# A state-space block with a mixture of experts on one core: the tail work of a unit is reordered, sums of squares move to ScalarE, and the end of the kernel is arranged anew

## What is computed

```python
x = x + conv(ln_c(x))        # conv: layer norm, mamba block, layer norm, projection
t = x as 4096 tokens
t = t + moe(ln_t(t))

def mamba(x):                # d_inner 128, state 16, 4 taps
    xi, z = split(x @ in_proj_w.T)
    xs = silu(causal_conv(xi)); dt, B, C = split(xs @ x_proj_w.T)
    delta = softplus(dt @ dt_proj_w.T + b)
    h[n] = exp(delta * A[n]) * h[n] + delta * xs * B[n]      # along 1024 tokens
    y = sum_n h[n] * C[n] + D * xs
    return (y * silu(z)) @ out_proj_w.T

def moe(x):                  # 8 experts, 640 places each, top 1
    e = argmax(x @ gate_w + gate_b); place = running count within e
    y = relu(x @ w1[e] + b1[e]) @ w2[e] + b2[e]
    return y * prob * (place < 640)
```

## Time and profile before

| | us |
|---|---|
| median of 3 runs | 411.19 (409.86 to 411.86) |
| the profiled execution, its own time | 404.2 |
| its span, first to last instruction | 402.4 |
| VectorE busy | 316.0 (79%) |
| TensorE busy | 314.5 (78%) |
| GpSimd busy | 269.3 (67%) |
| ScalarE busy | 225.2 (56%) |

### The profile page before, as it was taken

How to read it: one execution, slowest core, us unless ns; L and a number is a source line. 1 busy time by engine, 2 the same in 40 slices (tenths; PEclk the granted TensorE clock), 3 DMA queues, 4 the chain that set the end, 5 groups by cost and what they waited for, 6 DMA issues and landing times. The chain is left out here.

```text
span 402.4 us, 4213 instructions
## 1 busy us (share of the span) xinstructions
PE 314.5 (78%) x1257; PEld 187.1 (47%) x1257; DVE 316.0 (79%) x355; ACT 225.2 (56%) x398; POOL 269.3 (67%) x196
## 2 busy tenths in 40 slices
PE   8832988647988799898888959877678759999930
PEld 3311433113634355473434426544366536989920
DVE  4799998999997968999797899999997223565650
ACT  4456688718676944857885846455533226464410
POOL 3436847988564797688659768966588500777771
PEclk9975799998899955969996896999999559999975
DMA  5186999989987866588975638999801063000000
GB/s 105 29 290 242 266 294 402 374 201 377 368 261 285 241 197 252 195 247 280 329 241 187 222 135 281 284 329 340 156 21 31 15 189 81 9 16 17 21 11 0
DMA packets 43985, 78.67 MB, mean 195 GB/s; under 512 B 16051, under 2 KB 26094, under 8 KB 43963
## 3 DMA queue, kind: packets, MB, share of 16 engines
q1 hardware_dynamic: 41066, 73.88, 57.4%
q0 software_dynamic: 2896, 4.53, 4.0%
HBM read 72.30 MB, written 7.54 MB: 198 GB/s over the span
## 5 line engine op out<-in xcount | busy, mean ns | idle before, releaser
L481 POOL TENSOR_TENSOR prod<-h,csb 128x1024 f32<-128x1024 f32 (+1 forms) x64 | 142.0, 2221 | 55.5 <-DVE h L1217 33.4
L1217 DVE TENSOR_TENSOR_SCAN h<-dA,Bp 128x1024 f32<-128x1024 f32 (+1 forms) x64 | 137.7, 2151 | 4.8 <-ACT hl L661 1.4
L910 PE MATMUL Yp<-prod,ident 128*128 128x512 f32 (+1 forms) x256 | 128.3, 633 | 16.1 <-POOL prod L481 16.0
L647 ACT ACTIVATE dA<-delta,aneg 128x1024 f32<-128x1024 f32 (+1 forms) x64 | 69.0, 1090 | 29.8 <-DVE h L1217 25.5
L910 PEld LDWEIGHTS Yp<-prod,ident 128*128 128x128 f32 x256 | 50.0, 209 | 73.9 <-issue 46.5
L1187 DVE TENSOR_TENSOR Bp<-Cp,bsb 128x1024 f32<-128x1024 f32 (+1 forms) x64 | 74.6, 1166 | 3.5 <-DMA bsb<-bc_rows 1.4
L562 POOL DMA_INDIRECT out_dram<-dA,csb x30 | 30.7, 1023 | 28.1 <-DVE dA L1404 20.8
L520 POOL DMA_INDIRECT slots<-rows_,slot x30 | 30.1, 1005 | 7.2 <-issue 4.5
L1390 DVE TENSOR_TENSOR dA<-Bp,b2s 128x320 f32<-128x320 f32 x8 | 3.9, 491 | 26.2 <-PE Bp L1081 26.2
L1071 PE MATMUL Cp<-prod,w1s 128*128 128x384 f32 (+1 forms) x64 | 21.5, 459 | 0.0
L1081 PEld LDWEIGHTS Bp<-w2s,prod 128*128 128x128 f32 x160 | 19.0, 192 | 1.4 <-ACT prod L814 1.0
(11 more groups left out here) (276 smaller groups left out, 552.1 us busy)
## 6 DMA issues: line engine op xcount, KB each, us to landing
bsb<-bc_rows SPq DMA_DIRECT2D x48, 512.0 KB, 5.6
csb<-bc_rows SPq DMA_DIRECT2D x48, 512.0 KB, 5.8
bsb<-bc_rows SPq DMA_DIRECT2D x16, 384.0 KB, 4.7
csb<-bc_rows SPq DMA_DIRECT2D x16, 384.0 KB, 5.7
slots<-fill POOLq DMA_DIRECT2D x1, 2600.0 KB, 21.8
csb<-slots SPq DMA_DIRECT2D x6, 325.0 KB, 5.4
bcs<-bc_rows SPq DMA_DIRECT2D x2, 512.0 KB, 12.3
xs_in<-in_x_dram SPq DMA_DIRECT2D x1, 768.0 KB, 5.5
```

Source lines behind the costliest of these rows:

```text
L481: po.tensor_tensor(prod[:, k % 4, c], h[:, k % 3, c], csb[:, k % CSLOTS, c], ALU.mult).then_inc(s_pP, 1)
L647: ac.activation(dA[:, k % 3, c], at(delta, UNITS[v][0])[:, c], ACT.Exp, scale=aneg[:, n:n + 1]).then_inc(s_dA, 1)
L910: ins = te_.matmul(Yp[:, c], idn, prod[:, k % 4, c], start=False, stop=(n == 15), skip_group_check=True)
L1217: ve.tensor_tensor_scan(h[:, k % 3, c], dA[:, k % 3, c], Bp[:, c], 0.0, ALU.mult, ALU.add).then_inc(s_scan, 1)
```

## The change

1. **Squares.** Each `Square` of `back` (steps 2, 10, 11) becomes one activation per tile of 64 columns that also writes its sum (`accum_out`), and VectorE's two sums per unit go.
2. **Order of the back.** Both turned groups are evacuated at ScalarE's step 5; both groups of centred products are made at step 10, in one bank, and evacuated there; the second inverse root moves from step 13 to 12; ScalarE does `back` 9 before `front` 9. On TensorE, `back` 5 and `add_state` stand ahead of `front` 5. The logits get another bank; the wait for the gate's copies goes from TensorE to VectorE.
3. **The end of the scan.** The back of unit 3 runs ahead of the last pairs of unit 4; scatters and products stand in another order on GpSimd, one scatter of unit 3 now ahead of the last product; the zeroing of the lower half of `xT` on GpSimd and of `w1s` on VectorE go.
4. **The experts.** The first expert is finished in two blocks (three tiles and two, `FINISH`); the dense way runs eight chunks behind (`BEHIND`) instead of four; the place count of unit 4 (`back(LAST, 15)`) comes after the first `up`.

```diff
+FINISH = [(0, 0, 3), (0, 3, ET)] + [(e, 0, ET) for e in range(1, E)]
+BEHIND = 8
...
+        def products_bank(v, q, m):
+            if v < CARRY:
+                return M1[:, 4 * q * C:(4 * q + m) * C]
+            return turn_bank(v, q)[:, 0:m * C]
+        def turned_down(i):
+            e, k0, k1 = FINISH[i]
+            return (Yp if i == 1 else Bp)[:, HALF:HALF + (k1 - k0) * C]
+        def parts(v, n, first):
+            if v < CARRY:
+                return (0, 1) if n == first else ()
+            return (n - first,) if n in (first, first + 1) and quad(v, n - first) else ()
+        def logits(v, nt):
+            return (M1 if v < CARRY else Cp if v == CARRY else M0)[:, 0:nt * E]
...                                   GpSimd, end of the scan
-            for p in range(N // 2):
-                scatter(CARRY - 1, p, p + 1)
-                products(p)
-                if p == 0:
...
-                    po.memset(xT[C:P, :, :], 0.0).then_inc(e_zero, 1)
+            scatter(CARRY - 1, 0, 2)
+            products(0)
...
+            products(6)
+            scatter(CARRY, 0, 1)
+            products(7)
             back(LAST, 13)
-            scatter(CARRY, 0, UNITS[CARRY][2])
+            scatter(CARRY, 1, UNITS[CARRY][2])
...                                   ScalarE, back
                     act.wait_ge(b_op, v + 1)
-                    ac.activation(sq[:, 0:nt, :], tiles(mixer_bank(v)[:, 0:nt * C], C, nt), ACT.Square).then_inc(b_sq, 1)
+                    for t in range(nt):
+                        ins = ac.activation(sq[:, t, :], mixer_bank(v)[:, t * C:(t + 1) * C], ACT.Square, accum_out=bs[:, 0, t:t + 1])
+                    ins.then_inc(b_sq, 1)
...
-                    act.wait_ge(b_var, v + 1)
+                    act.wait_ge(b_sq, v + 1)
                     inverse_root(0, nt).then_inc(b_rs, 1)
...
-                if n in (5, 6) and quad(v, n - 5):
-                    q, w = n - 5, quad(v, n - 5) * P
+                for q in parts(v, n, 5):
...
-                    if v and n < 8:
+                    if v and n != 8 and n < 10:
                         back(v - 1, n)
                     if v + 1 < B:
                         front(v + 1, n)
-                    if v and n >= 8:
+                    if v and (n == 8 or n >= 10):
                         back(v - 1, n)
...                                   TensorE, steps of a unit
                 for n in range(16):
+                    if n == 5:
+                        if v:
+                            back(v - 1, n)
+                        add_state(v, n - 1)
                     if v + 1 < B:
                         front(v + 1, n)
...                                   VectorE, back
-                if n == 2:
-                    dve.wait_ge(b_sq, v + 1)
-                    ve.reduce_sum(bs[:, 0, 0:nt], sq[:, 0:nt, :], X).then_inc(b_var, 1)
...
-                if n == 12:
-                    dve.wait_ge(b_cg, quads(v + 1))
-                    ve.reduce_sum(bs[:, 10, 0:nt], sq[:, 0:nt, :], X).then_inc(b_var3, 1)
...                                   TensorE, experts
+                if i == 1:
                     down(0)
+                up(i)
+                if i == 0:
+                    back(LAST, 15)
+                if i == 1:
+                    down(1)
                 if i >= 4 and i % 2 == 0:
-                    down(i // 2 - 1)
-                if i >= 5:
-                    dense_down(i - 5)
+                    down(i // 2)
+                if i == BEHIND - 1:
+                    dense_turn()
+                if i >= BEHIND:
+                    dense_up(i - BEHIND)
```

More of the change, by code:

```diff
@@ L690, in back @@
                     ac.activation(bT[0:C, q * HALF:q * HALF + w], turn_bank(v, q)[0:C, 0:w], ACT.Copy).then_inc(b_h3T, 1)
[L691 to L695 removed]
+                for q in parts(v, n, 10):
+                    m = quad(v, q)
+                    act.wait_ge(b_lg, quads(v + 1) if v < CARRY else quads(v) + q + 1)
+                    src = tiles(products_bank(v, q, m), C, m)
+                    for t in range(m):
+                        ac.activation(sq[:, 4 * q + t, :], src[:, t, :], ACT.Square, accum_out=bs[:, 10, 4 * q + t:4 * q + t + 1])
                     ac.activation(cg[:, 4 * q:4 * q + m, :], src, ACT.Copy).then_inc(b_cg, 1)
[L697 to L698 removed]
+                if n == 12:
+                    act.wait_ge(b_cg, quads(v + 1))
                     inverse_root(10, nt).then_inc(b_rs3, 1)
@@ L706, in back @@
                                   bias=float(E * CAP)).then_inc(b_base, 1)
-                if n == (15 if v == CARRY else 13) and not last(v):
+                if n == 13 and not last(v):
                     act.drain()
@@ L793, in _ @@
                 decay_last(n)
-            back(CARRY, 2)
-            back(CARRY, 3)
+            for n in (2, 3, 5, 6):
+                back(CARRY, n)
             for n in range(12, N):
                 decay_last(n)
-            for n in (5, 6, 8, 9, 10, 11, 13, 14, 15):
+            for n in (8, 9, 10, 11, 12, 13, 14, 15):
                 back(CARRY, n)
@@ L1249, in back @@
                     dve.wait_ge(b_rs3, v + 1)
-                    link(ve.tensor_tensor(work(1, nt), work(0, nt), over(bs[:, 12, 0:nt], E), ALU.mult))
+                    if v + 2 < B:
+                        dve.wait_ge(f_zr, 2 * (v + 2))
+                    if v == CARRY:
+                        dve.wait_ge(b_cg, quads(v + 1))
+                    link(ve.tensor_tensor(work(1, nt), logits(v, nt).rearrange("p (t e) -> p t e", e=E),
+                                          over(bs[:, 12, 0:nt], E), ALU.mult))
                     link(ve.tensor_tensor(work(2, nt), work(1, nt), gb[:, :].unsqueeze(1).broadcast_to([P, nt, E]), ALU.add))
```

173 lines of the change are left out of this document (88 added, 85 removed).

## The result

The changed kernel takes 455.08 us (median of 4 runs, 454.52 to 455.41), the kernel before beside it on the same chip 410.52: ratio 1.116, 95% interval 1.111 to 1.121, so 44.6 us slower. The forecast was 404.4 us, faster. The profiled execution has a span of 453.4 us. First its page: the head, the slices of TensorE and of GpSimd, those of TensorE's granted clock, and the first line of the chain that ended last.

The account below looks back on a forecast made before the run. VectorE was taken to bound 29 to 288 us, then a chain through GpSimd and TensorE to the end. Units -1.3, end of scan -2.8, experts -2.7: -6.8 us from 411.19, so 404.4 us, range 398.8 to 410.5.

Parts of the forecast that it names:

- The experts: First turn to last output scatter: GpSimd's scatters become the bound from the second expert on; -2.7 us.
- the one with the low clock that stays: Rival: the clock falls at step 6 and does not come back; slower, 419 us with 18 us more low; chance 0.08.
- The tail of the dense way: End of the experts: TensorE's tail ends some 59 us behind the first turn, leaving 3 us of cover.
- Step 7: VectorE's wait for the projection in units 1 and 2: +1.6 us each, 3.1 more if the clock falls at step 6.
- one fall in each: Clock falls at one of two idle places in each of units 1 and 2: -0.5 and 0 us taken.
- all four falls: Rival: the clock falls at both places in units 1 and 2; units +4.3 us, whole 410.0; chance 0.15.
- the waits at step 13: VectorE's waits for the scaled logits in units 1 and 2; back 13 predicted at 153.2 to 156.6 in unit 1.
- the wait for `cg`: VectorE's wait for ScalarE's copy in units 1 and 2, 5.8 us in the two, predicted to go.
- The squares: ScalarE's squares with sums: 0.25 us each, between 0.16 and 0.35; about 3 us more ScalarE work per unit.
- The centring in one piece: Back of units 1 and 2 on TensorE: both groups' centrings together take 3.4 us.
- The end of the scan: First `drive_four` to the first expert's turn: last product 1.8 us later, first turn moves by -2.8 us.
- Unit 4: End of the scan: its back binds the first turn, its last pair 1.8 us late, TensorE free at about 324.9.

Follow-up runs that it names:

- e2_before_rows64: Kernel before with one edit, the experts' first product (`up`) on 64 rows instead of 128: 458.47 us, 1.125 of before.
- e1_rows128: Changed kernel with the experts' first product on 128 zero-padded rows again and both zeroing memsets back: 417.35 us, 1.014 of before.
- e4_rows128_old5: Changed kernel with 128 rows in the first product and the old order of step 5 (ScalarE's steps 8, 9 too): 401.26 us, 0.979 of before.
- g1_units_only: Kernel before with new sums, products in one piece and root at step 12 in units 0 to 2: 414.95 us, 0.986 of before.
- f2_rows96: e4_rows128_old5 with the experts' first product on 96 rows: 423.9 us (two runs), on a chip where the kernel before took 423.0.

## Why the prediction was wrong

- **The experts: the step that failed.** The sum took -2.7 there from the durations of before, at the full clock, since in the trace of before the clock comes back behind the first turn. It was +44.2. The prediction counted the zeroing (1.16 us on GpSimd) and never the product that reads the zeroed rows. No rival named it: the one with the low clock that stays placed it in the units. What the runs showed in its place: with `up` on 64 rows the clock stays at half for the whole stage, which cost 51 us put into the kernel before (`e2_before_rows64`) and gave 42 back taken out of the changed one (`e1_rows128`). With 128 rows the reasoning there held in kind. In `e4_rows128_old5` the scatters run without a wait from the second expert on, 347.22 to 391.63, and the last starts 65.80 behind the first turn, -0.4 for -2.7. The sizes missed: the second expert's first scatter came 21.4 behind the turn, not 19.8, and the scatters are 1.306 apart on the mean, not 1.275, which over 34 gaps is 1.1 us. The tail of the dense way had 5.3 us of cover (its store at 387.30, the end of the last scatter at 392.60), for the 3 that I gave it.
- **Step 7: right in mechanism, too small.** I had +1.6 from the later `Silu` and 3.1 more where the clock falls, 4.7. Measured: the waits are 5.8 and 5.7 longer. The table load ahead of the `Silu` stands at 122.58, behind an idle 1.56 for the second turn, and counted from ScalarE's last convolution output it is 2.15 us later than before, as predicted (2.1). The clock's share is 0.96 + 0.96 + 1.62 = 3.5 us (2.08, 2.08 and 3.52 less 1.12, 1.12 and 1.90). The rest, 2.3, is the 1.6 and 0.7 for the reduction that VectorE no longer does at step 2, which vanishes in this wait as I had said. The choice that failed is "one fall in each": it fell at both places in both units (behind an idle 3.29 us at 156 and at 231 a pair takes 2.98 and 3.11 for 1.88), and the waits at step 13 grew from 1.19 and 1.61 to 2.70 and 2.83, where my choice left none in unit 1. Of "all four falls" (+4.3 in the units, chance 0.15) the trace shows what I priced, but the units lost 10.25. (The sum has a slip there: unit 1 with both falls is -0.3 + 3.1 = +2.8, not +2.6.) By VectorE's waits up to the first `drive_four`, step 7 gave 11.5, step 13 2.7, the wait for `cg` -5.8. I hadn't counted a longer wait for `bsb` in unit 0 (2.86 for 1.37), one of 1.32 for unit 0's `yt`, and 1.4 more of scans that wait for their drive or decays. These make 12.6, and VectorE's busy time from 28 us on fell by 2.45: 10.2 in all.
- **The squares: 0.20 each, not 0.25.** The sum's read-out is an instruction of its own, started 0.10 behind the square, and eight take 1.60 us (below). The bounds 0.16 and 0.35 held it. The new sums without the order of step 5 gain 1.4% (`g1_units_only`).
- **The centring in one piece** took 1.89 us for 16 products at the full clock, where I had counted 3.4, twice the 1.70 that eight took before.
- **The end of the scan: nearly right.** The last product came 1.4 us later relative to the drive (predicted 1.8), the first turn -3.75 (predicted -2.8) and -3.0 in `e4_rows128_old5`. Unit 4 didn't bind: the loads of `slots` did. Its logits ended 33.8 us behind the drive, not 36.5 (the 324.9 of the prediction): its last pair came 0.6 later than before and not 1.8, and the two groups behind the pair took 0.66 each for 1.11, at the full clock; the rest of its back ran at half as before (its projection 1.12 in both). Where the clock is down in the first 25 us behind the drive, the gain is gone.

## What to carry to other kernels

Read an operand's shape in a diff as a possible change of TensorE's clock, not only of its data: a product over half the rows lasted as long at a given clock, and cost 12% of this kernel through the clock. Zero rows that a change drops as needless may be what lets the clock return; test such an edit by itself. And work moved from a gap on TensorE to ahead of it leaves the gap bare: having the second turn and a pair in the gap behind the `Silu` was worth 10 us.

## What the runs showed of the hardware that was not expected

TensorE stayed at 1.2 GHz (0.50) from the first turn to the end, busy for 50 of 50 us in the window above, while a third of its work (40.0 of 124 us, summed over the forms) was `up` on 64 rows; with 128 rows there, the added ones zeros, it came back to 1.00 within 4 to 6 us of the first turn (`e1_rows128`, `e4_rows128_old5`), with 96 within 16 (`f2_rows96`). With 72 it came back 38 us behind the first turn, at 364, fell at 381 and stayed down. What it is about the rows that counts, no run here shows. A square with its sum on ScalarE is two instructions, here in the changed kernel's timeline:

```profile
107.61 0.23 ACT L701 ACTIVATE sq<-M 128x64 f32<-128x64 f32 x1 [0.73 <-PE M L961]
107.73 0.20 ACT L701 ACTIVATION_READ_ACCUMULATOR sq<-M 128x1 f32 x1
107.83 0.22 ACT L701 ACTIVATE sq<-M 128x64 f32<-128x64 f32 x1
...
109.20 0.65 ACT L704 ACTIVATE y<-M 128x512 f32<-128x512 f32 x1
```
